# A third buffer for swapped products and for turned blocks in block 1's attention, and the fetch of turned probabilities one tick later

## What is computed

```
def _rope(x, sin, cos):
    xe = x[..., ::2]; xo = x[..., 1::2]
    re = xe * c - xo * s
    ro = xe * s + xo * c
    return jnp.stack((re, ro), axis=-1).reshape(x.shape)

q = _rope(heads(xq @ wq)); k = _rope(heads(k_in)); sim = q k^T * 64 ** -0.5
a = softmax(sim); o = a v; return o @ wo + bo
```

## Time and profile before

| | |
|---|---|
| median of 3 runs | 4076.74 us (4074.68 to 4083.11) |
| profiled execution | 4081.0 us, its span 4079.2 us |
| PE busy | 3852.5 us, 94% of the span |
| DVE busy | 3158.6 us, 77% |
| POOL busy | 2864.6 us, 70% |
| ACT busy | 2465.3 us, 60% |
| granted TensorE clock | 0.992 of full speed on the mean |
| DMA, SyncE's queue | 539.03 MB, 41.9% of the time of 16 engines |
| SW<-SN | 1024 transfers of 128 KB, 2.7 us from issue to landing (median) |
| p_scratch<-TR | 256 of 512 KB, 3.4 us |
| PB<-p_scratch | 1024 of 128 KB, 3.1 us |

### The profile page before, as it was taken

One profiled execution on the slowest core, in us unless ns is written; L12 is line 12 of the kernel. 1 busy time (PEld: TensorE's weight loads), 2 busy tenths in 40 slices (PEclk: granted clock), 3 DMA queues, 4 the chain that ended last, 5 costly groups with the idle time before them and its releaser, 6 DMA issues.

```text
span 4079.2 us, 92937 instructions
## 1 busy us (share of the span) xinstructions
PE 3852.5 (94%) x32822; PEld 3294.9 (81%) x32822; DVE 3158.6 (77%) x6610; ACT 2465.3 (60%) x10244; POOL 2864.6 (70%) x2674
## 2 busy tenths in 40 slices
PE   7999999999989999999999999899999999999999
PEld 6777777777779997888888888777777877778998
DVE  7888889999875557878878787888888888875443
ACT  6999998888963344555555555555555555554333
POOL 5777777777767776666666666677676777766776
PEclk9999999999999999999999999999999999999999
DMA  2101111111111123676766667666666676773110
GB/s 81 31 29 33 33 46 48 48 39 42 53 60 42 45 81 125 206 221 200 223 207 215 209 206 232 208 208 217 207 220 215 211 223 208 223 226 96 49 45 32
DMA packets 415216, 544.98 MB, mean 134 GB/s; under 512 B 58524, under 2 KB 311968, under 8 KB 414752
## 3 DMA queue, kind: packets, MB, share of 16 engines
q1 hardware_dynamic: 414684, 539.03, 41.9%
q10 hardware_dynamic: 68, 0.02, 0.0%
HBM read 220.11 MB, written 184.55 MB: 99 GB/s over the span
## 4 chain that ended last, share of the span: by engine, by line
PE 45%; DVE 14%; POOL 11%; issue 9%; DMA 9%; ACT 8%; SPq 4%; ACTq 0%; POOLq 0%; DVEq 0%
PE BANKS L628 11%; PE BANKS L629 10%; PE BANKS L630 10%; ACT PR L926 5%; DMA p_scratch<-TR 5%; POOL PR L1265 4%; PE BANKS L708 3%; PE BANKS L823 3%; DMA PB<-p_scratch 2%; POOL KT L1284 2%; PE BANKS L787 2%; PE BANKS L775 2%; SPq L601 2%; POOL QT L1284 2%; DVE SN L1146 2%
## 5 line engine op out<-in xcount | busy, mean ns | idle before, releaser
L1265 POOL TENSOR_TENSOR PR<-PR,RL 128x512 f32<-128x512 f32 x1024 | 1065.7, 1044 | 523.4 <-DVE RL L1078 522.2
L942 ACT ACTIVATE PR<-BANKS,NM 128x128 f32<-128x128 f32 x2048 | 719.4, 377 | 541.7 <-DVE NM L1132 541.7
L926 ACT ACTIVATE PR<-BANKS,NM 128x128 f32<-128x128 f32 x2048 | 728.6, 414 | 12.7 <-DVE NM L1065 10.5
L628 PE MATMUL BANKS<-HH,WH 128*128 128x512 f32 x1632 | 681.6, 418 | 2.1 <-ACT HF L969 1.6
L629 PE MATMUL BANKS<-HL,WH 128*128 128x512 f32 x1632 | 642.6, 394 | 0.0
L630 PE MATMUL BANKS<-HH,WL 128*128 128x512 f32 x1632 | 641.7, 393 | 0.0
L926 ACT ACTIVATION_READ_ACCUMULATOR PR<-BANKS,NM 128x1 f32 x2048 | 521.2, 255 | 0.0
L1146 DVE TENSOR_TENSOR SN<-BANKS,ROPE 128x512 f32<-128x512 f32 x512 | 348.4, 681 | 129.5 <-DMA SW<-SN 128.8
L942 ACT ACTIVATION_READ_ACCUMULATOR PR<-BANKS,NM 128x1 f32 x2048 | 443.1, 216 | 0.0
L1085 DVE STREAM_TRANSPOSE TR<-PR 128x512 f32<-128x512 f32 x512 | 351.6, 687 | 101.9 <-DMA p_scratch<-TR 56.7
L628 PE MATMUL BANKS<-WH,OH 128*128 128x256 f32 x1280 | 378.8, 296 | 37.1 <-DVE OL L1150 31.8
(11 more groups left out here) (134 smaller groups left out, 10667.3 us busy)
## 6 DMA issues: line engine op xcount, KB each, us to landing
SW<-SN SPq DMA_DIRECT2D x1024, 128.0 KB, 2.7
p_scratch<-TR SPq DMA_DIRECT2D x256, 512.0 KB, 3.4
PB<-p_scratch SPq DMA_DIRECT2D x1024, 128.0 KB, 3.1
x_scratch<-X SPq DMA_DIRECT2D x80, 512.0 KB, 3.3
X<-x_scratch SPq DMA_DIRECT2D x80, 512.0 KB, 4.2
CX<-in_ctx SPq DMA_DIRECT2D x32, 384.0 KB, 4.2
X<-in_x SPq DMA_DIRECT2D x16, 512.0 KB, 4.0
out<-X SPq DMA_DIRECT2D x16, 512.0 KB, 2.9
```

The source lines that it names most:

```text
L628: e.matmul(o, lh, rh, start=first and i == 0, stop=False)
L926: made = e.activation(pr[:, r], bank[:, r], ACT.Exp, bias=nm[:, h:h + 1], accum_out=RL[npr(t)[0]][:, h:h + 1])
L942: made = e.activation(pr[:, r], bank[:, r], ACT.Exp, bias=nm[:, h:h + 1], accum_out=RL[npr(t)[0]][:, h:h + 1])
L1265: e.tensor_tensor(p3, p3, RL[npr(t)[0]][:, :].unsqueeze(2).broadcast_to([128, 4, 128]), ALU.mult).then_inc(s_nrm, 1)
```

## The change

SW and TR get a third buffer each, and the fetch (`get`) moves from lag 5 to lag 6, so that in SyncE's even tick it follows the store of the next unit and precedes the KT swap. The waits follow the number of buffers: a swap waits for addition r - 3, a VectorE product still waits until the swap two products back has landed, now under that swap's own semaphore. SHARED, the memory that block 0's probabilities and block 1's buffers share, grows from 512 * 11 to 512 * 13 columns, and `dynamic_dma_scratch_size` falls from 2048 to 256 bytes per partition.

```diff
@@ -16,7 +16,7 @@
 NSTG = 3
 NH = 3
 NP0, NPT0 = 5, 6
-NP1, NTR, NPT1, NSC = 4, 2, 3, 4
+NP1, NTR, NSW, NPT1, NSC = 4, 3, 3, 3, 4
 
 CONTEXT = ("Wk", "Wv", "ck", "cv")
 
@@ -196,7 +196,7 @@
                 for j in range(8):
                     x = Unit(unit, p, g, j)
                     tick = tg + 2 * j
-                    for stage, lag in (("q1", -5), ("q1_add", -3), ("k1", -4), ("k1_add", -2), ("scores", 0), ("max", 0), ("put", 4), ("get", 5),
+                    for stage, lag in (("q1", -5), ("q1_add", -3), ("k1", -4), ("k1_add", -2), ("scores", 0), ("max", 0), ("put", 4), ("get", 6),
                                        ("pv", 8), ("low", 8), ("out", 9)):
                         at[stage, tick + lag].append(x)
                     at["v1", tick + 1].append((p, g, j))
@@ -281,10 +281,9 @@
             PT = [sb(f"PT{i}", [128, 512], stack=soft) for i in range(NPT0)]
         with spare:
             sb("PR_L1", [128, 512 * NP1], stack=spare)
-            SW = [sb("SW0", [128, 512], stack=spare)]
+            SW = [sb(f"SW{i}", [128, 512], stack=spare) for i in range(NSW)]
             TR = [sb(f"TR{i}", [128, 1024], stack=spare) for i in range(NTR)]
-            SW += [sb("SW1", [128, 512], stack=spare)]
-        sb("SHARED", [128, 512 * (NP0 + NPT0)])
+        sb("SHARED", [128, 512 * (NP1 + NSW + 2 * NTR)])
         CX = sb("CX", [128, G, 256])
         PB = [sb(f"PB{i}", [128, 4, 256]) for i in range(NPT1)]
         with first:
@@ -352,7 +351,7 @@
             sem(k) for k in ("s0", "nm0", "s", "nm", "exp", "rl", "nrm", "t", "pt_a", "pt_d", "pv0", "pv"))
         s_oh, s_ol, s_y = sem("oh"), sem("ol"), sem("y")
         s_qk, s_rt, s_zz, s_v1, s_va = (sem(k) for k in ("qk", "rt", "zz", "v1", "va"))
-        s_sw = [sem(f"sw{i}") for i in range(2)]
+        s_sw = [sem(f"sw{i}") for i in range(NSW)]
         s_tr = sem("tr")
         s_put = [sem(f"put{i}") for i in range(NTR)]
         s_get = [sem(f"get{i}") for i in range(NPT1)]
@@ -603,9 +602,9 @@
                     for x in at[stage, tick]:
                         r = 2 * x.i + w
                         q.wait_ge(s_rt, r + 1)
-                        q.wait_ge(s_zz, r - 1)
+                        q.wait_ge(s_zz, r - NSW + 1)
                         for i in range(2):
-                            e.dma_start(SW[r % 2][i:128:2, :], SN[r % 2][1 - i:128:2, :]).then_inc(s_sw[r % 2], 16)
+                            e.dma_start(SW[r % NSW][i:128:2, :], SN[r % 2][1 - i:128:2, :]).then_inc(s_sw[r % NSW], 16)
                 done = [(x.p, x.g) for x in at["res0", tick] if x.b == G - 1]
                 done += [(x.p, x.g) for x in at["out", tick - 1] if x.j == 7]
                 done += [(p, g) for p, g, j in at["down", tick - 1] if j == 7]
@@ -1142,7 +1141,7 @@
                         q.wait_ge(s_rope, 16)
                         e.tensor_tensor((QT, KT)[w][x.i % 3][:, :].rearrange("p (b t) -> p b t", b=G), src, cs, ALU.mult)
                         if r >= 2:
-                            q.wait_ge(s_sw[r % 2], 32 * (r // 2))
+                            q.wait_ge(s_sw[(r - 2) % NSW], 32 * ((r - 2) // NSW + 1))
                         e.tensor_tensor(SN[r % 2][:, :].rearrange("p (b t) -> p b t", b=G), src, sn, ALU.mult).then_inc(s_rt, 1)
 
                 for x in at["low", tick]:
@@ -1280,8 +1279,8 @@
                     for x in at[stage, tick]:
                         r, z = 2 * x.i + w, (QT, KT)[w][x.i % 3]
                         q.wait_ge(s_rt, r + 1)
-                        q.wait_ge(s_sw[r % 2], 32 * (r // 2 + 1))
-                        e.tensor_tensor(z[:, :], z[:, :], SW[r % 2][:, :], ALU.add).then_inc(s_zz, 1)
+                        q.wait_ge(s_sw[r % NSW], 32 * (r // NSW + 1))
+                        e.tensor_tensor(z[:, :], z[:, :], SW[r % NSW][:, :], ALU.add).then_inc(s_zz, 1)
 
                 for p, g, j in at["up", tick]:
                     f = ffj(p, g, j)
@@ -1349,7 +1348,7 @@
     import concourse.bacc as bacc
     from concourse.bass_utils import run_bass_kernel_spmd
 
-    nc = bacc.Bacc("TRN2", target_bir_lowering=False, num_devices=1, dynamic_dma_scratch_size=2048)
+    nc = bacc.Bacc("TRN2", target_bir_lowering=False, num_devices=1, dynamic_dma_scratch_size=256)
     arrays, aps = {}, {}
     for name, arr in [(n, inputs[n]) for n in _INS] + list(_constants().items()):
         arr = np.ascontiguousarray(arr)
```

## The result

The changed kernel takes 4189.2 us (median of 4 runs, 4183.0 to 4190.3) against 4079.3 us before, a ratio of 1.027 with a 95% interval of 1.025 to 1.029. I had forecast 4017 us, with 4112 us as the price of the slower rival.

The account below looks back on a forecast made before the run. TensorE was taken to bound block 1's attention, with 121 us of excess; gains of 30 us (self-attention) and 29 us (cross-attention), say 60, gave 4017 us against the median, range 3980 to 4085 us.

Parts of the forecast that it names:

- slower rival: Block 1's attention: fetch is the bound, landing 1.9 us later each time; 4112 us, chance 0.16.
- The floor and what bounds the kernel: Block 1's attention: TensorE's own work sets the floor, 7.97 us per self-attention unit and 7.66 us per cross-attention unit.
- my excess: Unit periods above TensorE's floor: 38 us in the self-attention, 83 us in the cross-attention, the most the change could bring.
- Third SW, third TR: SyncE's 339.2 us of KT-addition waits nearly all go; VectorE's transpose waits for stores go, at no cost.
- The 60 us that I forecast: Net gain of the whole change: 30 us in the self-attention and 29 us in the cross-attention, rounded.
- The KT waits that follow: Cross-attention: GpSimd's HL pair delays the KT addition, costing the scores 1.4 us more once per group, 22 us.
- The fetch at lag 6: SyncE's queue: 233.4 us of store waits go; the price is the fetch's cover, 32 us in the cross-attention.
- the fetch's cover: Slack from VectorE's QT product to TensorE's value product: 0.8 us in the self-attention, -0.5 us in the cross-attention.
- The clock: Cross-attention: half-clock moments behind the 0.98 clock were taken as already counted in the unit periods.
- the argument that I put against it: Against the slower rival: most fetches before also waited for their store, and so started late anyway.

Follow-up runs that it names:

- e11: e10 with, in addition, VectorE's OL difference ahead of the products for QT, KT and SN; 3978.4 us, ratio 0.974.
- e1: The changed kernel with the fetch back at lag 5, so only the third SW and third TR remain; 4014.3 us, ratio 0.983.
- e7: The changed kernel with the fetch at lag 5 and two TR, so only the third SW remains; 4019.0 us, ratio 0.985.
- e8: The changed kernel with the fetch at lag 5 and two SW, so only the third TR remains; 4081.8 us, ratio 1.000.
- e10: e1 with GpSimd's rotary additions ahead of the HL differences of the same tick; 3998.9 us, ratio 0.979.
- e6: The changed kernel with context and weight loads issued behind store and fetch; 4125.1 us, ratio 1.010.
- e5: The changed kernel with the fetch ahead of the next unit's store but still behind the loads; 4065.4 us, ratio 0.995.
- e3: The changed kernel with the fetch still at lag 6 but issued first in SyncE's tick; 4026.8 us, ratio 0.986.
- e9: The changed kernel with the store cut to 64 partitions, 256 KB, from the fifth unit on; 4136.5 us, ratio 1.013.
- e12: The changed kernel with the store cut to 16 partitions, 64 KB, from the fifth unit on; 4096.1 us, ratio 1.003.

## Why the prediction was wrong

- **The floor and what bounds the kernel: right.** e11 reaches 7.64 us in the cross-attention against 7.66; e1 has 7.93 us in the self-attention (840.9 / 106 by the same copy) against 7.97. But the 8.27 us of the self-attention held the join of the stages; its steady part was 8.10 us, so 22 us of my excess lay at the join and not in the regular units.
- **Third SW, third TR: right by themselves.** SyncE's lateness on GpSimd's addition was the cause of the PB waits: with the third SW the 339.2 us fall to 21.0 us (e1), and with it alone 64 of the 67 us come back (e7). Beside the later fetch 164.5 us of that wait stay. The 60 us that I forecast were the net of the whole change, so that their nearness to the 67 us of the buffers is no hit. That TR's waits would go at no cost was right, but e8 shows that they were worth nothing.
- **The KT waits that follow: right in kind.** I wrote 22 us more than the 9.3 us of before, once per group; e1 shows 22.7 us in all, in 16 waits, and e10 removes them by order alone. In the changed kernel they stayed at 10.1 us, since PB came later still.
- **The fetch at lag 6: this step failed, in its price, the fetch's cover.** I had left 0.8 us of cover in the self-attention and a shortfall of 0.5 us in the cross-attention, 32 us in all; the move cost 175 us. Three terms were wrong. (1) I moved the fetch past the store and the QT swap only. In the tick that it enters, SyncE also issues the context loads and the weight loads, with their waits for VectorE. They were in the code and not in my sum: 64 us beside the store (e6), 39 us without it (e5 against e3). (2) The way from the QT product to the fetch was right, 3.06 us (2098.84 to 2101.90) against my 1.38 + 1.10 + 0.59 = 3.07, and so was the landing behind the store, 3.8 us at most in that unit and 3.5 us on the median against the 3.8 us of rows 15. The issues were not: I took 1.74 us for the four from one unit, and they take 2.3 us in every other self-attention unit and 2.65 and 3.91 us in those between. Only a part of that is the store's (e5). (3) I took the room from a unit whose QT product is 1.29 us ahead of the value product. At the sixth unit of each group it is 0.48 us, as it was before (2088.32 and 2088.82), since VectorE does other work first; I had granted such lateness only to the cross-attention. At that unit the room is 0.48 + 7.82 = 8.3 us, 9.0 us had to go into it, and the cover is -0.7 us, not +0.8; at the others the long issues of (2) are what it lacks. The store's data alone are worth some 106 us (e9, e12).
- **The clock.** I counted it inside the periods of before. But the longer waits go with half-clock stretches of their own: 0.54 for 7 us after a wait of 2.86 us, and 0.97 over 850 us of the cross-attention, against 0.99 before and 1.00 in e1. 0.03 x 850 = 26 us of that stretch's clock time are lost against e1, an estimate, as the shares are rounded.
- **The slower rival** named the place, the fetch as the bound, and its price of 4112 us was 77 us short. Its term was another one, though, a landing 1.9 us later each time; the landing grew by some 0.5 us. It had 0.16. The argument that I put against it, that fetches before started late anyway, was wrong: they started late and had a tick more to do so.

Still open is why one of the four issues takes so long at every second unit of the self-attention: it does so with and without the store ahead (3.91 us for the four in the changed kernel, 3.22 us in e5), and no run here isolates it.

## What to carry to other kernels

When a transfer is moved in an in-order queue, list everything that the queue issues in the slot it enters, per-group loads and their waits included; an issue order inside a tick can be worth more (162 us here) than the tick itself (13 us). A transfer that somebody waits for goes ahead of those that nobody waits for soon, and the larger these are the more it matters. And try the parts of a change apart: here one was worth 67 us and the other lost 175 us.

## What the runs showed of the hardware

- The cost of the transfer ahead in the same queue went with its size in the two sizes tried: 0.21 us of the total per KB over about 250 units, or 0.8 ns per KB and unit, 0.4 us per unit for 512 KB. The fetch's own landing grew with it: 3.0 us on the median behind 64 KB (and with the store behind the fetch), 3.2 us behind 256 KB, 3.5 us behind 512 KB.
- Four fetches of 128 KB took 1.74 and 1.93 us to issue in the kernel before and 1.96 us in e5, ahead of the store; behind 512 KB it was 2.28 us. At every second unit of the self-attention it was 2.65 and 3.91 us in the changed kernel and 3.22 us in e5, for a reason that stays open.
- After a wait of 2.86 us TensorE's granted clock was 0.54 over the next 7 us, most of it at 1.2 GHz, so that the stall cost about twice what the wait shows: by estimate 7 x 0.46 = 3.2 us more.
